# An embedding sum with a small MLP: table 0 fetched row by row by two engines, and the last tables turned in halves

## What is computed

```
emb = jax.vmap(lambda tab, idx: tab[idx])(tables, cat_features)
emb_btd = jnp.transpose(emb, (1, 0, 2))
wide_num = jax.nn.relu(numerical @ w_wide + b_wide)
cat_sum = jnp.sum(emb_btd, axis=1)
linear_output = cat_sum + wide_num
x = jnp.concatenate([numerical, emb_btd.reshape(numerical.shape[0], T * D)], axis=1)
x = jax.nn.relu(x @ W1 + b1)          # 3341 -> 256
x = jax.nn.relu(x @ W2 + b2)          # 256 -> 128
dnn_output = x @ W3 + b3              # 128 -> 1
return jax.nn.sigmoid(dnn_output + linear_output)
```

## Time and profile before

| what | value |
|---|---|
| median of 3 runs | 142.7 us (142.04 to 145.11) |
| the profiled execution | 141.84 us |
| its span, first to last instruction | 140.1 us |
| mean granted PE clock, share of full speed | 0.976 |
| busy PE / POOL / ACT / DVE | 102.4 / 96.4 / 20.5 / 5.8 us |
| DMAs of single rows issued by SP / by ACT | 256 / 128 |
| gathers issued by POOL | 101 |

### The profile page before, as it was taken

How to read it: one execution, slowest core, us unless ns; L and a number is a source line. 1 busy time by engine, 2 the same in 40 slices (tenths; PEclk the granted TensorE clock), 3 DMA queues, 4 the chain that set the end, 5 groups by cost and what they waited for, 6 DMA issues and landing times.

```text
span 140.1 us, 1840 instructions
## 1 busy us (share of the span) xinstructions
PE 102.4 (73%) x386; PEld 59.6 (43%) x386; DVE 5.8 (4%) x22; ACT 20.5 (15%) x42; POOL 96.4 (69%) x108
## 2 busy tenths in 40 slices
PE   0594299965859488568549567939959999788991
PEld 0224265531435144324315332435445655446880
DVE  2400100000000000000000000000000000002221
ACT  0400011110111011011101100101110221113431
POOL 2777877778777777777777777777777777777000
PEclk9999999999999999999999999986977999999999
DMA  3989954532355665562452443442623612223210
GB/s 88 316 283 267 234 93 48 57 61 58 51 53 60 59 42 61 55 62 59 49 68 51 50 59 54 43 73 48 56 61 49 48 55 59 56 48 63 39 42 19
DMA packets 9246, 10.84 MB, mean 77 GB/s; under 512 B 3018, under 2 KB 7619, under 8 KB 9235
## 3 DMA queue, kind: packets, MB, share of 16 engines
q0 software_dynamic: 3232, 6.63, 36.6%
q1 hardware_dynamic: 4624, 3.80, 9.3%
q10 hardware_dynamic: 1379, 0.29, 1.2%
HBM read 10.45 MB, written 0.26 MB: 76 GB/s over the span
## 4 chain that ended last, share of the span: by engine, by line
POOL 61%; issue 20%; PE 10%; DMA 3%; ACT 1%; POOLq 1%; DVE 1%; ACTq 0%
POOL emb L197 61%; PE first_layer L287 4%; PE mlp L299 2%; DMA emb<-in_L_rec_tables,row_idx 2%; DMA first_cat<-in_r_cat_features 2%; PE first_layer L263 1%; PE total L293 1%; ACT late_t L412 1%; POOLq L47 1%; PE turn L278 1%; PE total L258 1%; PE turn L246 0%; PE total L307 0%; ACT y L421 0%; DVE h L373 0%
## 5 line engine op out<-in xcount | busy, mean ns | idle before, releaser
L197 POOL DMA_INDIRECT emb<-in_L_rec_tables,row_idx x100 | 94.3, 943 | 30.5 <-issue 30.5
L263 PE MATMUL first_layer<-emb_t,w 128*128 128x512 f32 x96 | 48.9, 633 | 3.0 <-ACT emb_t L404 2.9
L246 PE MATMUL turn<-ident,emb 128*128 128x128 f32 x96 | 16.5, 298 | 23.4 <-DMA emb<-in_L_rec_tables,row_idx 23.4
L404 ACT COPY emb_t<-turn 128x512 f32<-128x512 f32 x24 | 14.1, 586 | 101.9 <-PE turn L246 88.8
L246 PEld LDWEIGHTS turn<-ident,emb 128*128 128x128 f32 x96 | 11.4, 148 | 40.1 <-DMA emb<-in_L_rec_tables,row_idx 36.9
L258 PE MATMUL total<-emb,ident 128*128 128x256 f32 x96 | 27.4, 412 | 0.0
L263 PEld LDWEIGHTS first_layer<-emb_t,w 128*128 128x128 f32 x96 | 17.8, 203 | 21.3 <-issue 13.5
L258 PEld LDWEIGHTS total<-emb,ident 128*128 128x128 f32 x96 | 18.0, 209 | 1.6
L368 DVE TENSOR_SCALAR h<-first_layer,vec_cols 128x128 f32<-128x128 f32 x4 | 1.4, 350 | 116.9 <-PE first_layer L287 116.9
L287 PE MATMUL first_layer<-late_t,w 128*128 128x128 f32 x32 | 5.4, 292 | 1.2 <-ACT late_t L412 0.8
L287 PEld LDWEIGHTS first_layer<-late_t,w 128*128 128x128 f32 x32 | 4.2, 190 | 2.5 <-ACT late_t L412 2.5
(11 more groups left out here) (35 smaller groups left out, 17.8 us busy)
## 6 DMA issues: line engine op xcount, KB each, us to landing
emb<-in_L_rec_tables SPq DMA_DIRECT2D x256, 0.5 KB
w<-in_L_rec_W SPq DMA_DIRECT2D x2, 1152.0 KB, 12.5
emb<-in_L_rec_tables ACTq DMA_DIRECT2D x128, 0.5 KB
emb<-in_L_rec_tables,row_idx POOLq DMA_INDIRECT x100, 3.7
w<-in_L_rec_W SPq DMA_DIRECT2D x1, 768.0 KB, 5.3
w<-in_L_rec_W SPq DMA_DIRECT2D x1, 256.0 KB, 2.9
out<-y SPq DMA_DIRECT2D x4, 64.0 KB, 1.7
w<-in_L_rec_W ACTq DMA_DIRECT2D x1, 128.0 KB
```

The source lines that it names most:

```text
L197: nc.gpsimd.indirect_dma_start(emb[:, t, c, :], None, rows, bass.IndirectOffsetOnAxis(ap=index, axis=0)).then_inc(landed, 16)
L246: mm = nc.tensor.transpose(turn[step % 2][:, chunk(c)], emb[:, t, c, :], ident[:, :])
L263: mm = nc.tensor.matmul(first_layer[k][:, :], w1[:, t, chunk(k)], emb_t[:, step % SLOTS, :], start=False, stop=False, skip_group_check=True)
L404: nc.scalar.copy(emb_t[:, step % SLOTS, :], turn[step % 2][:, :]).then_inc(copied, 1)
```

## The change

Tile (0,0) is no longer gathered: SP fetches (0,0) and (0,2) row by row, and ACT (0,1) and (0,3), 256 rows each. POOL issues 100 gathers, and its first one is tile (1,0). ACT issues twelve rows behind each part that PE has turned, and no longer copies: DVE does the copies of the tables (a new L396). The work on tables 0 to 23 becomes a list `PARTS` of 27 parts: tables 1 to 15 whole, the first half of table 0 (chunks 0 and 1), tables 16 to 21 whole, the second half of table 0, and tables 22 and 23 in two halves each. The two late tiles of a chunk are added on DVE (`sum_late`), so that PE adds one tile to `total` for a chunk (`add_late`) in place of two.

```diff
+HALVED = 2
-BY_SYNC = [(0, 2), (0, 3)]
-BY_SCALAR = [(0, 1)]
+BY_SYNC = [(0, 0), (0, 2)]
+BY_SCALAR = [(0, 1), (0, 3)]
-ROWS_A_STEP = 8
+ROWS_A_STEP = 12
...
-    ORDER = [*range(1, BODY - 3), 0, *range(BODY - 3, BODY)]
+    WHOLE = BODY - 1 - HALVED
+    PARTS = [(t, 0, CH) for t in range(1, WHOLE - 5)] + [(0, 0, CH // 2)]
+    PARTS += [(t, 0, CH) for t in range(WHOLE - 5, WHOLE + 1)] + [(0, CH // 2, CH)]
+    PARTS += [(t, lo, lo + CH // 2) for t in range(WHOLE + 1, BODY) for lo in range(0, CH, CH // 2)]
+    LAST = len(PARTS)
...
+            def turn_part(i):
+                t, lo, hi = PARTS[i]
+                if by_pool(i):
+                    pe.wait_ge(gathered[i], 16 * by_pool(i))
+                if i >= 2:
+                    pe.wait_ge(copied, i - 1)
+                for c in range(lo, hi):
                     if (t, c) in fetched:
                         pe.wait_ge(fetched[t, c], 16 * P)
+                    mm = nc.tensor.transpose(turn[i % 2][:, chunk(c)], emb[:, t, c, :], ident[:, :])
                 mm.then_inc(turned, 1)
...
-                nc.tensor.matmul(total_of(c), ident[:, :], emb[:, BODY + g, c, :],
+                nc.tensor.matmul(total_of(c), ident[:, :], late_sum[:, c, :],
                                  start=False, stop=False, skip_group_check=True)
...
+            for i, (_, lo, hi) in enumerate(PARTS):
+                cols = slice(lo * P, hi * P)
+                dve.wait_ge(turned, i + 1)
+                if i >= SLOTS:
+                    dve.wait_ge(used, i - SLOTS + 1)
+                nc.vector.tensor_copy(emb_t[:, i % SLOTS, cols], turn[i % 2][:, cols]).then_inc(copied, 1)
...
+            def sum_late(c):
+                for n in range(c * LATE, (c + 1) * LATE):
+                    dve.wait_ge(late_gathered[n], 16)
+                nc.vector.tensor_tensor(late_sum[:, c, :], emb[:, BODY, c, :], emb[:, BODY + 1, c, :], ALU.add
+                                        ).then_inc(late_summed, 1)
...
-            for step in range(BODY):
-                act.wait_ge(turned, step + 1)
-                if step >= SLOTS:
-                    act.wait_ge(used, step - SLOTS + 1)
-                nc.scalar.copy(emb_t[:, step % SLOTS, :], turn[step % 2][:, :]).then_inc(copied, 1)
-                for t, c, b in places[step * ROWS_A_STEP:(step + 1) * ROWS_A_STEP]:
+            for i in range(LAST):
+                act.wait_ge(turned, i + 1)
+                for t, c, b in places[i * ROWS_A_STEP:(i + 1) * ROWS_A_STEP]:
                     if b % REGS == 0:
                         regs = load_places(act, t, c, b)
                     fetch_row(act, regs.pop(0), t, c, b)
```

More of the change, by code:

```diff
@@ L31, in build, with rows_apart, part_of, by_pool @@
     ROW = D * 4
-    assert B == CH * P and D == P and H2 == P and KH == 2 and T * CH <= P and W1_CUTS[-1] == T
-    ORDER = [*range(1, BODY - 3), 0, *range(BODY - 3, BODY)]
[L36 to L41, removed]
+    assert LATE == 2 and B == CH * P and D == P and H2 == P and KH == 2 and T * CH <= P and W1_CUTS[-1] == T
+    assert all(t == 0 for t, c in BY_SYNC + BY_SCALAR)
+    WHOLE = BODY - 1 - HALVED
[3 more added lines that the diff above has]
+    LAST = len(PARTS)
+    assert sum(hi - lo for t, lo, hi in PARTS) == BODY * CH and PARTS[0][1:] == (0, CH)
+    def rows_apart(t, c):
+        return (t, c) in BY_SYNC + BY_SCALAR
+    BODY_TILES = [(t, c) for t, lo, hi in PARTS for c in range(lo, hi) if not rows_apart(t, c)]
+    FIRST = BODY_TILES[0][0]
+    def part_of(t, c):
+        return next(i for i, (u, lo, hi) in enumerate(PARTS) if u == t and lo <= c < hi)
+    def by_pool(i):
+        t, lo, hi = PARTS[i]
+        return sum(not rows_apart(t, c) for c in range(lo, hi))
     rows = tables.rearrange("t v d -> (t v) d")
@@ L96, in build @@
         h2 = sb("h2", [H2, B])
+        late_sum = sb("late_sum", [P, CH, D])
         y = sb("y", [P, CH, D])
@@ L130, in build @@
         wide_ready = sem("wide_ready")
-        gathered = {t: sem(f"gathered{t}") for t in ORDER}
+        gathered = [sem(f"gathered{t}_{lo}") for t, lo, hi in PARTS]
         turned = sem("turned")
@@ L139, in build @@
         late_copied = sem("late_copied")
+        late_summed = sem("late_summed")
         h1_low_done = sem("h1_low_done")
@@ L167, in _ @@
             with nc.allow_non_contiguous_dma(reason="one index for each partition"):
-                sp.dma_start(first_cat[:, :], cat[0:1, 0:P].rearrange("a p -> p a")).then_inc(first_loaded, 16)
+                sp.dma_start(first_cat[:, :], cat[FIRST:FIRST + 1, 0:P].rearrange("a p -> p a")).then_inc(first_loaded, 16)
             for i, loaded in enumerate(w1_loaded):
@@ L203, in _ @@
             gp.wait_ge(first_steps, 3)
-            gather(0, 0, first_row[:, :], gathered[0])
+            gather(FIRST, 0, first_row[:, :], gathered[part_of(FIRST, 0)])
             gp.wait_ge(rows_ready, 1)
             for t, c in BODY_TILES[1:]:
-                gather(t, c, column(t, c), gathered[t])
+                gather(t, c, column(t, c), gathered[part_of(t, c)])
             for n in range(TILES):
@@ L236, in _ @@
                                 ident[0:KH + 2, 0:KH + 2]).then_inc(vecs_turned, 1)
[L238 to L243, removed]
+            def turn_part(i):
+                t, lo, hi = PARTS[i]
+                if by_pool(i):
[3 more added lines that the diff above has]
+                for c in range(lo, hi):
                     if (t, c) in fetched:
                         pe.wait_ge(fetched[t, c], 16 * P)
-                    mm = nc.tensor.transpose(turn[step % 2][:, chunk(c)], emb[:, t, c, :], ident[:, :])
+                    mm = nc.tensor.transpose(turn[i % 2][:, chunk(c)], emb[:, t, c, :], ident[:, :])
                 mm.then_inc(turned, 1)
@@ L253, in wait_w1, with sum_part @@
                     seen.add(part)
[L255 to L259, removed]
+            def sum_part(i):
+                t, lo, hi = PARTS[i]
+                cols = slice(lo * P, hi * P)
+                for j in range(2):
+                    own = range(lo + (lo + j) % 2, hi, 2)
+                    if own:
+                        nc.tensor.matmul(total[j][:, own[0] // 2 * P:(own[-1] // 2 + 1) * P], ident[:, :],
+                                         emb[:, t, own[0]:hi:2, :], start=(i == 0), stop=False, skip_group_check=True)
                 wait_w1(t)
-                pe.wait_ge(copied, step + 1)
+                pe.wait_ge(copied, i + 1)
                 for k in range(KH):
-                    mm = nc.tensor.matmul(first_layer[k][:, :], w1[:, t, chunk(k)], emb_t[:, step % SLOTS, :],
+                    mm = nc.tensor.matmul(first_layer[k][:, cols], w1[:, t, chunk(k)], emb_t[:, i % SLOTS, cols],
                                           start=False, stop=False, skip_group_check=True)
                 mm.then_inc(used, 1)
-            for step in range(BODY):
-                turn_table(step)
-                sum_table(step)
+            for i in range(LAST):
+                turn_part(i)
+                sum_part(i)
             def turn_tile(n):
@@ L273, in turn_tile @@
                 pe.wait_ge(late_gathered[n], 16)
-                if n < 2:
-                    pe.wait_ge(copied, BODY - 1 + n)
-                else:
+                if n >= 2:
                     pe.wait_ge(late_copied, n - 1)
@@ L290, in sum_tile, with add_late @@
                         mm.then_inc(done, 1)
-                if c >= 2 and g == 0:
+            def add_late(c):
+                pe.wait_ge(late_summed, c + 1)
+                if c >= 2:
                     pe.wait_ge(y_ready, c - 1)
-                nc.tensor.matmul(total_of(c), ident[:, :], emb[:, BODY + g, c, :],
+                nc.tensor.matmul(total_of(c), ident[:, :], late_sum[:, c, :],
                                  start=False, stop=False, skip_group_check=True)
@@ L313, in _ @@
                 if c >= 1:
+                    add_late(c - 1)
                     layer2(c - 1)
@@ L319, in _ @@
                 sum_tile(n + 1)
+            add_late(CH - 1)
             layer2(CH - 1)
@@ L341, in _ @@
             dve.wait_ge(first_steps, 2)
-            nc.vector.tensor_tensor(first_row[:, :], first_neg[:, :], first_lim[:, :], ALU.add
-                                    ).then_inc(first_steps, 1)
+            nc.vector.scalar_tensor_tensor(first_row[:, :], first_neg[:, :], float(FIRST * V), first_lim[:, :],
+                                           ALU.add, ALU.add).then_inc(first_steps, 1)
             dve.wait_ge(cat_steps, 2)
@@ L374, in relu_h2 @@
                                         ).then_inc(h2_ready, 1)
+            def sum_late(c):
[3 more added lines that the diff above has]
+                                        ).then_inc(late_summed, 1)
             for c in range(CH):
+                sum_late(c)
                 relu_h1_high(c)
```

## The result

The changed kernel takes 156.93 us in the median (156.32 to 158.09, 4 runs), the kernel before 142.37 (141.89 to 145.11, 4 runs). The ratio is 1.104 with a 95% interval of 1.098 to 1.110: 10% slower, where the forecast was 149.4 and the range ended at 153.0. The span of the profiled execution went from 140.1 to 155.7 us.

What follows compares the result with a forecast made beforehand. POOL's gathers and pauses were taken to bound the kernel before; after, ACT's late rows: landing 122.3 + half parts 9.1 + clock 1.6 + late tiles 14.6 = 147.6 span, plus 1.74 outside, 149.4 us; range 145.0 to 153.0.

Steps and rivals of the forecast that it cites:

- What bounds the kernel, and the gather less: POOL's gathers up to table 23: one fewer ends them 1.25 us earlier, worth nothing if ACT is late.
- 256 rows on ACT: ACT's queue: starts at 17.4, works 103.0 us without idling, issues its last row at 120.4 (116.7 to 122.9).
- The landing of the last row: Last row of (0,3): lands 2.1 us after issue at 120.2, at 122.3; up to 3.7 later at the high end.
- Table 21 "is worked off by about 116": PE before table 0's second half: table 21 lands 3.7 after 107.67, then PE stands still some 6 us.
- Rival A: ACT keeps up, its rows landing before PE has done table 21: 140.8 us (139.7 to 142.5), not slower; chance 0.09.
- Five half parts and the clock: PE from the last row's landing to the first late tile: five halves of 1.81, 9.1 us, plus 1.6 for slow clock.
- The late tiles: From the first late tile to the span's end: four sums of 0.22 saved, 14.6 us in place of 15.5.
- Copies on DVE: Table copies: 0.68 against 0.59 us, 0.09 more a table, hidden behind the gathers and not holding up POOL.
- Rival B: Copies on DVE lock POOL out of its gathers, 16.7 us if each whole copy stops it: time 155; chance 0.03.

Runs made afterwards that it cites:

- e5: The changed kernel with ACT's 128 rows of (0,3) sent to a tile nobody reads; PE turns zeros without waiting: 150.79 us in the median.
- e7: The kernel before with only its table copies moved from ACT to DVE: 142.08 us, ratio 1.0001.
- e12: The changed kernel with (0,0) gathered, SP fetching (0,2) and (0,3), ACT (0,1), nine rows a part, table 0's second half ahead of table 21: 140.61 us.
- e16: The kernel of e5 with ten rows of ACT behind each part in place of twelve: 151.90 us, ratio 1.069.
- e6: The changed kernel without issuing ACT's 128 rows of (0,3), zeros turned in their place: 142.59 us, ratio 0.998.

## Why the prediction was wrong

The direction and the first mechanism were right; the forecast was short by 8.1 us of span (147.6 against 155.7). Step by step:

**What bounds the kernel, and the gather less.** Right. POOL's gathers stayed 1.25 us apart, the last of table 23 went one place earlier, and nothing came of it.

**256 rows on ACT.** The start was right: 19.45 less a load of 2.24 is 17.2, forecast 17.4. The work was 106.2 us, forecast 103.0. The rate was right: ACT's rows stood 0.325 apart, SP's 0.322, and with eight loads of 2.24 that makes 101.1. Mis-sized was what stands around them, as these rows of the chain show:

```profile
106.07 0.31 issue
106.38 0.23 ACTq L177
...
110.55 2.24 ACTq L172
...
112.88 0.47 ACTq L177
113.44 0.23 ACTq L177
```

The first row behind each load takes 0.47 to issue in place of 0.23, 1.9 us for eight, and at seven other rows ACT paused for 0.3 to 0.6, 2.8 together; the forecast had 1.0, for the waits. ACT had no pause longer than that, as forecast. Last issue 123.2 in place of 120.2: 3.0 of the 8.1. The load of 2.2 us held, against the 600 ns that the Trainium skill ("DMA: Bandwidth & Descriptors", "Latency and other measured facts") gives as its floor.

**The landing of the last row** is the step that failed: 2.1 us forecast from a DMA that was the first in its queue, 7.33 measured, 5.2 of the 8.1. Its bound, 3.7, failed too. SP had issued its last row 14 us before, at 109.0, and the row was late all the same, as were the gathers issued beside it (7.5 in the median from 119 to 130). The term was priced from an empty queue, and the load that the change itself makes was put at nothing.

**Table 21 "is worked off by about 116".** Wrong by almost 10 us, PE being through at 125.9: a landing of 3.7 was assumed, the median of a kernel in which ACT issues half as many rows; it was 13.3. That this cost nothing in the sum is luck: the wait for rows came later still. But it voids Rival A: e5 takes ACT's rows off PE's path and gives 148.4 to 151.2, not 140.8. That rival asked only how fast ACT is; neither it nor any other case priced what the rows do to the gathers. A hint was in the trace of before: its median landing falls from 3.3 to 2.6 us once SP's rows end at 109.

**Five half parts and the clock.** Forecast 10.7 us from the landing to the first late tile, measured 141.11 - 130.57 = 10.5. A half took 1.87 (139.25 - 137.38) in place of 1.81. The granted clock fell to 0.64 of full speed in the first half part and 0.68 in the second and was 1.00 from the third on; those two took 2.7 and 2.2, 1.2 more for 1.6 forecast.

**The late tiles.** Forecast 14.6 to the end of the span, measured 155.7 - 141.1 = 14.6.

**Copies on DVE.** Hidden, as forecast: e7 has the ratio 1.0001, with 24 copies of 0.69. Rival B falls, and the trace of e7 agrees, now on more than one copy, with the section "Who interferes with whom" of the Trainium skill's "SBUF — State Buffer".

## What to carry to other kernels

When a queue gets more DMAs, ask twice: how long will it issue, and what will its traffic do to the transfers that other queues have under way. Take the price of a landing from a stretch with the load that the change makes; if there is none, the upper end is open, and the range must say so. An engine's issue is more than its rows times their distance: count the first one behind each load and the pauses, and count what stands behind them in its queue.

## What the runs showed of the hardware

- SP issued 25 single rows of 512 bytes in 10 us in the kernels before and after (256 in 102; 103 to 104 us in e12 and e16). With ACT issuing 25 in 10 us beside it (256 in 104), POOL's gathers landed up to 13.3 us behind their issue, growing up to 109 us; at 22 to 24 (e16) 8.4; at 20 (e12) the longest fell from 7.0 to 4.1, at 18 (before, 128 in 70) from 6.0 to 4.2. It was gone within about 10 us of ACT's end (e6).
- By the count of packets, about one in sixteen of each gather was late (33 open in the mean from 115 to 120 us, against 26).
- The rows themselves land late as well, 7.33 us for the last.
- A DMA of a row into 2, 4 or 16 separate pieces takes ACT's queue 0.54 to 0.58 us in place of 0.23, whatever their number, and the first row behind a load of 32 registers 0.47.
- Chips differ: on some the issue of a row took about 2.8 us, up to 140 us, in place of 0.32, and the kernel before took 1.8 times as long.
